# Causal self-attention in a two-layer decoder: reciprocals and maxima at later steps, and the mask of the second scores moved from TensorE to GpSimd

## The chip, the cores and the metric

The kernel runs on one core of one Trainium2 chip. The metric is the device time of one execution in microseconds (us), the median of three runs; less is better.

## The reference

Two decoder layers with normalisation behind each part, on x of 4 x 1024 x 256. Only the first part of the first layer is touched by the change: causal self-attention with 16 heads of 16 features.

```python
qkv = x @ w_in.T + b_in
q, k, v = split(qkv, 3)                       # 16 heads of 16
scores = einsum('bhqd,bhkd->bhqk', q / 4, k)
scores = scores + where(tril(ones((1024, 1024))), 0.0, -inf)
attn = softmax(scores)
out = einsum('bhqk,bhkd->bhqd', attn, v) @ w_out.T + b_out
x = layernorm(x + out)
```

Behind it come cross-attention, a quantised feed-forward block with a convolution, and the second layer (attention, cross-attention, feed-forward). They use other buffers and begin when the first part is done.

## The kernel before

The program is written engine by engine: inside each engine's function stands its own list of instructions in order, and semaphores tie the lists together. Each engine takes its instructions strictly in that order, so a wait holds all that stands behind it. SP (SyncE) issues all DMAs of this part.

**Groups, tiles and steps.** The 4 batches have 4 groups of 4 heads each: 16 groups. Sequence positions are cut in 8 tiles of 128. A group is gone through twice. The first pass (`first_scores`, L390 to L403) makes the scores of one query tile against all keys up to it in psA, adds a mask to the diagonal block by a product of identb and masku (L401), and VectorE takes the maximum of each row (L721, written negated to negm). The second pass (`second_scores`, L405 to L414) makes the scores of one key tile against all later queries in psB, with keys on the partitions; three additional rows of qst carry the negated maxima. ScalarE takes exp into pbuf (L535), and TensorE multiplies with V (`values`, L416 to L432) into psO, where an additional column of ones gives the denominators. psA, psB and psO have two halves each; pbuf has two buffers, one for odd and one for even key tiles.

A common step number k runs from 0 to 138 on all engines. Step k does a first-pass query tile of group k // 8, the second-pass key tile of step s = k - 10, and the product with V of the key tile of s - 1. Key tiles come in the order 3, 2, 1, 0, 7, 6, 5, 4, so that steps with k % 8 = 2 have key tile 3, those with k % 8 = 7 key tile 6, with k % 8 = 0 tile 5, with k % 8 = 1 tile 4. A step is made of rounds: one unit of second scores (up to 512 columns), some first scores, and in round 0 or 1 a product with V. c is the half of the queries (0 to 511, 512 to 1023) that a product is for.

**The mask of the second pass.** Where key tile and query tile are the same, queries ahead of the key must not see it. L413 adds to that block of 128 x 128 the product of identb and maskl, which is -1e30 there, so that exp makes zeros: one matmul for each head and key tile, 512 in all.

**Maxima.** At the end of each step with k % 8 = 7 TensorE transposes the maxima of the group (L477), VectorE splits them into three bfloat16 parts (`split_max`, L647 to L655), and SP stores them (L335) and loads them as rows of qst (L337). The second pass of the group begins at k % 8 = 2.

**Denominators.** At step 8g + 19 SP runs `reciprocals(g)` (L257 to L275): it stores the denominators of group g out of OT, moves OT to OTC, loads the denominators spread over 128 partitions, waits for VectorE's reciprocal (L687, on VectorE at step 8g + 20), stores the inverses and loads them broadcast to rden (four DMAs, L274). For odd g GpSimd multiplies OTC with rden (L573) at step 8g + 21.

**Other work in these steps.** The projections to q and k of the next batch (`qk_unit`: even steps 2 to 16 of 32; TensorE L368, ScalarE L508 and L514, GpSimd L558 to L566, SP L239), the projection to V (steps 24 to 31 of 32), the output projection of the batch before with residual and statistics (`out_unit`, steps 16 to 23 of 32; GpSimd L579 and L580), and GpSimd's rounding of the feed-forward weights (`quantise`, steps 18 to 28), on which SP's loads of later weights (L301 to L308, step 31) wait.

## Time and profile before

| | |
|---|---|
| median of 3 runs | 2337.58 us (2334.3 to 2339.44) |
| profiled execution | 2344.96 us |
| its span in the trace | 2343.2 us |
| PE busy | 2013.2 us, 86% of the span |
| DVE busy | 1439.8 us, 61% |
| ACT busy | 1207.0 us, 52% |
| POOL (GpSimd) busy | 726.3 us, 31% |
| the part that is changed | from 0 to about 782 us of the span |

PE is TensorE, PEld its weight loads, DVE VectorE, ACT ScalarE, SP SyncE. A matmul's duration counts its way through the array, and matmuls on end overlap: what one costs in a row of them is the distance of their starts. In square brackets stands how long the engine was idle before, and what released it.

### The profile page before, as it was taken

Reading aid. Unit: us, or ns where it says so; the run is one execution under the profiler, and the core shown is the slowest. Engines: PE = TensorE matmul, PEld = TensorE weight load, DVE = VectorE, ACT = ScalarE, POOL = GpSimd, SP = SyncE. Lnnn points to the kernel's source line nnn. Section 1 sums busy time; section 2 is a strip of 40 time slices with the busy share of each in tenths; the row PEclk is TensorE's granted clock in tenths of the full one; section 3 lists DMA queues with packets and bytes.
Section 4 is the critical chain, followed back from the end, with each engine's and each line's share of the span. In section 5 each row is a group of like instructions: output and inputs, shape, how many; then the busy total and the mean of one; then the engine's idle time right before and its main releaser. Section 6 shows DMA issues by size and latency. Waiting matters only on the chain. (4 is left out here: it accounts for less than half of the span.)

```text
span 2343.2 us, 32739 instructions
## 1 busy us (share of the span) xinstructions
PE 2013.2 (86%) x11274; PEld 1122.7 (48%) x11274; DVE 1439.8 (61%) x2698; ACT 1207.0 (52%) x2758; POOL 726.3 (31%) x1040
## 2 busy tenths in 40 slices
PE   6899799889998589999999985989899967798886
PEld 3344344334342345555555553556566643344444
DVE  4665576566773365666887985494844345567655
ACT  2355445544655166555787781557642314364352
POOL 4251220120010200021553551384833322343323
PEclk8899999999998799999999998999999978899998
DMA  6536433543531200000111013110001156645321
GB/s 153 118 66 151 81 64 83 92 83 66 75 58 39 67 22 5 28 26 8 55 53 43 35 44 145 53 46 10 30 28 52 45 118 125 125 86 113 79 63 41
DMA packets 134471, 156.56 MB, mean 67 GB/s; under 512 B 38446, under 2 KB 104882, under 8 KB 134211
## 3 DMA queue, kind: packets, MB, share of 16 engines
q1 hardware_dynamic: 134306, 154.48, 28.7%
q8 instruction: 91, 1.49, 0.3%
q14 instruction: 74, 0.60, 0.1%
HBM read 99.16 MB, written 46.86 MB: 62 GB/s over the span
## 5 line engine op out<-in xcount | busy, mean ns | idle before, releaser
L535 ACT ACTIVATE pbuf_sb<-psB 128x512 f32<-128x512 f32 (+1 forms) x608 | 330.2, 573 | 267.5 <-PE psB L413 216.2
L721 DVE TENSOR_REDUCE negm_sb<-psA 128x1 f32<-128x640 f32 (+6 forms) x352 | 351.8, 1027 | 180.5 <-PE psA L401 173.6
L1263 ACT ACTIVATE pw_sb<-psA,nmx_sb 128x154 f32<-128x154 f32 x512 | 192.3, 390 | 133.3 <-DVE nmx_sb L1408 133.3
L410 PE MATMUL psB<-qst_sb,kst_sb 99*128 99x512 bf16 (+3 forms) x768 | 239.3, 342 | 16.7 <-issue 6.3
L399 PE MATMUL psA<-kst_sb,qst_sb 96*128 96x512 bf16 (+3 forms) x768 | 201.6, 339 | 26.3 <-DVE negm_sb L721 25.3
L1408 DVE TENSOR_REDUCE nmx_sb<-psA 128x4 f32<-128x616 f32 x128 | 102.0, 797 | 124.6 <-PE psA L1032 124.2
L427 PE MATMUL psO<-pbuf_sb,V_sb 128*32 128x512 f32 (+3 forms) x1536 | 166.2, 513 | 11.0 <-ACT OT_sb L521 8.9
L410 PEld LDWEIGHTS psB<-qst_sb,kst_sb 99*128 99x128 bf16 x768 | 76.1, 100 | 183.7 <-ACT pbuf_sb L535 127.4
L2940 DVE TENSOR_REDUCE negm_sb<-psA 128x2 f32<-128x320 f32 x256 | 116.3, 481 | 71.2 <-PE psA L2703 69.6
L2823 ACT ACTIVATE pb_sb<-psB 128x512 f32<-128x512 f32 x160 | 93.4, 600 | 117.8 <-PE psB L2713 113.3
L985 PE MATMUL psO<-XT_sb,wq_x_sb 128*128 128x512 f32 x256 | 121.0, 596 | 0.0
L2703 PE MATMUL psA<-kst_sb,qst_sb 97*128 97x160 bf16 x512 | 83.3, 250 | 42.4 <-DVE negm_sb L2940 34.6
L985 PE MATMUL psO<-wo_x_sb,ox_sb 128*128 128x256 f32 x512 | 117.3, 383 | 1.7 <-DVE famw_sb L1494 0.9
L2052 PE MATMUL psO<-va_sb,pat_sb 128*128 128x256 f32 x512 | 115.9, 379 | 1.0 <-DVE pat_sb L2493 1.0
L2052 PE MATMUL psA<-XT_sb,ka_sb 128*128 128x512 f32 x256 | 116.8, 599 | 0.0
L558 POOL TENSOR_TENSOR q_sb<-q_sb,parts_sb 128x512 f32<-128x512 f32 x32 | 37.8, 1181 | 242.9 <-ACT parts_sb L514 242.7
L2466 DVE TENSOR_REDUCE nma_sb<-psA 128x1 f32<-128x1024 f32 x32 | 39.1, 1222 | 117.5 <-PE psA L2052 117.5
L399 PEld LDWEIGHTS psA<-kst_sb,qst_sb 96*128 96x128 bf16 x768 | 70.6, 101 | 80.7 <-DVE negm_sb L721 43.3
L401 PE MATMUL psA<-masku_sb,identb_sb 128*128 128x128 bf16 x512 | 108.6, 226 | 0.0
L2052 PEld LDWEIGHTS psO<-va_sb,pat_sb 128*128 128x128 f32 x512 | 96.9, 190 | 22.6 <-issue 7.7
L1046 PE MATMUL psB<-ident_sb,pr_sb 128*128 128x128 f32 x512 | 83.6, 286 | 26.6 <-DVE pt_sb L1401 26.5
L985 PEld LDWEIGHTS psO<-wo_x_sb,ox_sb 128*128 128x128 f32 x512 | 97.4, 192 | 17.3 <-ACT ox_sb L1198 1.7
(306 smaller groups left out, 4317.3 us busy)
## 6 DMA issues: line engine op xcount, KB each, us to landing
qst_sb<-parts_dram SPq DMA_DIRECT2D x192, 128.0 KB, 4.5
parts_dram<-parts_sb SPq DMA_DIRECT2D x32, 384.0 KB, 2.6
kst_sb<-parts_dram SPq DMA_DIRECT2D x96, 128.0 KB, 7.6
OTC_sb<-OT_sb SPq DMA_DIRECT2D x128, 64.0 KB, 5.7
rden_sb<-dens_dram SPq DMA_DIRECT2D x128, 64.0 KB, 2.2
x_dram<-X_sb SPq DMA_DIRECT2D x64, 128.0 KB, 1.7
y_dram<-yw_sb SPq DMA_DIRECT2D x16, 512.0 KB, 2.8
Y_sb<-y_dram SPq DMA_DIRECT2D x16, 512.0 KB, 9.0
```

What stands on the lines that cost most here:

```text
L399: nc.tensor.matmul(psA[:, k, at + lo:at + hi], qst[0:QK_ROWS, gg % 3, h, j * P:(j + 1) * P], kst[0:QK_ROWS, gg % 3, h, lo:hi], start=True, ...
L401: last = nc.tensor.matmul(psA[:, k, at + w - P:at + w], identb[:, :], masku[:, :], start=False, stop=True)
L410: last = nc.tensor.matmul(psB[:, k, at:at + hi - lo], kst[0:MAX_ROWS, gg % 3, h, i * P:(i + 1) * P], qst[0:MAX_ROWS, gg % 3, h, lo:hi], st ...
L427: last = nc.tensor.matmul(psO[32 * h:32 * h + 32, c, lo - c * 512:hi - c * 512], V[:, b % 2, i, at:at + 32], pbuf[:, i % 2, h, lo:hi], sta ...
L535: nc.scalar.activation(pbuf[:, key % 2, heads[0]:heads[-1] + 1, lo:hi], psB[:, (nb.n - 1) % 2, 0:len(heads) * (hi - lo)] .rearrange("p (h ...
L721: nc.vector.tensor_reduce(out=negm[:, gg % 2, heads[0]:heads[-1] + 1, j], in_=psA[:, (na.n - 1) % 2, :].rearrange("p (h n) -> p h n", h=le ...
L985: last = nc.tensor.matmul(dst, lhsT(i), rhs(i), start=(i == 0), stop=(i == n - 1))
L1263: last = nc.scalar.activation(pw[:, m % 2, h, :], psA[:, m % 2, at:at + K], ACT.Exp, bias=nmx[:, m % 2, h:h + 1], accum_out=psx[:, m % 3, ...
L1408: nc.vector.tensor_reduce(out=nmx[:, m % 2, :].rearrange("p (b a) -> p a b", a=2), in_=psA[:, m % 2, :].rearrange("p (a n) -> p a n", a=2) ...
L2052: last = nc.tensor.matmul(dst, lhsT(i), rhs(i), start=(i == 0), stop=(i == n - 1))
L2823: nc.scalar.activation(pb1[:, v % 2, h, :], psB[:, (nb.n - 1) % 2, :], ACT.Exp).then_inc(b_free, 1)
L2940: nc.vector.tensor_reduce(out=negm1[:, gg % 2, 2 * half:2 * half + 2, j], in_=psA[:, 0, half * 512:half * 512 + 2 * KP].rearrange("p (a n) ...
```

## The change

Line numbers below are those of the old file. The change
- drops maskl and its 512 products (L413); GpSimd sets the future part of each diagonal block of pbuf to zero instead, one `affine_select` of 128 x 4 x 128 for each step of the second pass (`clear_future`, 128 in all, the first thing GpSimd does in a step), and the product with V that reads this block waits for it (`future_cleared`);
- puts the product with V for c = 1 in round 1 rather than 0 where its key tile is 4 to 7;
- puts the transpose of the maxima behind round 0 of the next step, and `split_max` at the beginning of the next step on VectorE;
- splits SP's `reciprocals`: the inverses are stored and loaded four steps later, behind the maxima of that step; VectorE's reciprocal goes two steps later, GpSimd's scaling three, the output projection two;
- cuts GpSimd's rounding of weights in pieces of 512 columns over the steps 18 to 29;
- has ScalarE copy psO to OT before it stores the projection to q and k.

```diff
@@ -125,7 +125,6 @@
     masku = sb("masku", [P, P], BF16, first_stage)
-    maskl = sb("maskl", [P, P], BF16, first_stage)
     qst = sb("qst", [P, 3, 4, S], BF16, first_stage)
@@ -166,6 +165,7 @@
     inv_stored, inv_loaded, ot_scaled = sem0("f_inv_stored"), sem0("f_inv_loaded"), sem0("f_ot_scaled")
+    future_cleared = sem0("f_future_cleared")
     var_ready, rstd_ready, x_ready, x_stored = sem0("f_var_ready"), sem0("f_rstd_ready"), sem0("f_x_ready"), sem0("f_x_stored")
@@ -208,7 +208,7 @@
         b, kk = k // 32 - 1, k % 32
-        return (b, kk - 16) if 0 <= b < B - 1 and 16 <= kk < 24 else None
+        return (b, kk - 18) if 0 <= b < B - 1 and 18 <= kk < 26 else None
@@ -219,6 +219,13 @@
                             + bool(v_unit(i)) + bool(out_unit(i)) for i in range(k))
+
+    def diagonal_exps(s):
+
+        i = KEY_ORDER[s % 8]
+        before = 8 + sum((len(second_units(KEY_ORDER[(k - LEAD) % 8])) if k >= LEAD else 0) + bool(qk_unit(k))
+                         for k in range(s + LEAD))
+        return before + sum(lo == i * P for _, lo, _ in second_units(i))
@@ -253,7 +260,7 @@
-            def reciprocals(gg):
+            def denominators(gg):
@@ -264,6 +271,9 @@
                 sp.dma_start(dens[:, :], dens_dram[0].rearrange("h (a n) -> (h a) n", a=P // 4)).then_inc(dens_loaded, 16)
+
+            def inverses(gg):
+
                 sp.wait_ge(inv_made, gg + 1)
@@ -296,7 +306,7 @@
-                sp.wait_ge(quantised, 2)
+                sp.wait_ge(quantised, 8)
                 for dst, name in ((wk_x0, "L0_xattn_WkT"), (wv_x0, "L0_xattn_WvT"), (wq_x0, "L0_xattn_WqT")):
@@ -329,20 +339,23 @@
                 if early_groups(k) is not None:
-                    reciprocals(early_groups(k))
+                    denominators(early_groups(k))
                 if k < UNITS and k % 8 == 7:
...
                                  max_dram[gg % 2].rearrange("a (h j) n -> a h (j n)", h=4)).then_inc(maxrows_loaded, 16)
+                if early_groups(k - 4) is not None:
+                    inverses(early_groups(k - 4))
                 if k >= 2 and out_unit(k - 2):
...
                     sp.dma_start(X0[:, :, :], t["x"][b].rearrange("(n p) d -> p n d", p=P)).then_inc(x_loaded, 16)
-            reciprocals(G * B - 1)
+            denominators(G * B - 1)
+            inverses(G * B - 1)
             for j in range(NT):
@@ -406,11 +419,9 @@
                 for a, h in enumerate(heads):
-                    at, diagonal = a * (hi - lo), lo == i * P
+                    at = a * (hi - lo)
                     last = nc.tensor.matmul(psB[:, k, at:at + hi - lo], kst[0:MAX_ROWS, gg % 3, h, i * P:(i + 1) * P],
-                                            qst[0:MAX_ROWS, gg % 3, h, lo:hi], start=True, stop=not diagonal)
-                    if diagonal:
-                        last = nc.tensor.matmul(psB[:, k, at:at + P], identb[:, :], maskl[:, :], start=False, stop=True)
+                                            qst[0:MAX_ROWS, gg % 3, h, lo:hi], start=True, stop=True)
                 last.then_inc(b_full, 1)
@@ -419,6 +430,8 @@
                 pe.wait_ge(b_free, seen)
+                if c == i // 4:
+                    pe.wait_ge(future_cleared, 8 * gg + KEY_ORDER.index(i) + 1)
                 if i == KEY_ORDER[0] and gg > 0:
@@ -430,6 +443,13 @@
                     last.then_inc(pv_done, 1)
+
+            def transpose_maxima(gg):
+
+                pe.wait_ge(a_free, na.n)
+                a = slot_a()
+                nc.tensor.transpose(psA[0:32, a, 0:P], negm[:, gg % 2, :, :].rearrange("p h j -> p (h j)"),
+                                    ident[:, :]).then_inc(a_full, 1)
@@ -454,8 +474,10 @@
                         first_scores(k // 8, first[f], query_tile(k))
-                    if u == 0 and s >= 1:
+                    if u == (KEY_ORDER[(s - 1) % 8] >= 4) and s >= 1:
                         values((s - 1) // 8, KEY_ORDER[(s - 1) % 8], exps_at[s - 1], 1)
+                    if u == 0 and k % 8 == 0 and 8 <= k <= UNITS:
+                        transpose_maxima(k // 8 - 1)
                     if u == 1 and s >= 1:
@@ -471,11 +493,6 @@
                     nc.tensor.matmul(psA[:, a, 0:2], ones[:, :], asum[:, :], start=True, stop=True).then_inc(a_full, 1)
-                if k < UNITS and k % 8 == 7:
-                    pe.wait_ge(a_free, na.n)
-                    a = slot_a()
-                    nc.tensor.transpose(psA[0:32, a, 0:P], negm[:, (k // 8) % 2, :, :].rearrange("p h j -> p (h j)"),
-                                        ident[:, :]).then_inc(a_full, 1)
                 if v_unit(k):
@@ -535,13 +552,13 @@
                                              .rearrange("p (h n) -> p h n", h=len(heads)), ACT.Exp).then_inc(b_free, 1)
-                if qk_unit(k):
-                    store_qk(*qk_unit(k))
                 if s >= 0:
...
                         copy_out(gg, 0)
+                if qk_unit(k):
+                    store_qk(*qk_unit(k))
             copy_out(G * B - 1, 1)
@@ -579,17 +596,23 @@
+            def clear_future(s):
+
+                key = KEY_ORDER[s % 8]
+                pool.wait_ge(b_free, diagonal_exps(s))
+                nc.gpsimd.affine_select(out=pbuf[:, key % 2, :, key * P:(key + 1) * P],
+                                        in_=pbuf[:, key % 2, :, key * P:(key + 1) * P], compare_op=ALU.is_ge, fill=0.0,
+                                        base=0, pattern=[[0, 4], [1, P]], channel_multiplier=-1).then_inc(future_cleared, 1)
+
             link(nc.gpsimd.memset(ones[:, :], 1.0))
             link(nc.gpsimd.memset(mhalf[:, :], -0.5))
-            for m in (ident, identb, masku, maskl):
+            for m in (ident, identb, masku):
                 link(nc.gpsimd.memset(m[:, :], 0.0))
...
                                          base=0, pattern=[[-1, P]], channel_multiplier=1))
-            link(nc.gpsimd.affine_select(out=maskl[:, :], in_=maskl[:, :], compare_op=ALU.is_ge, fill=MASKED,
-                                         base=0, pattern=[[1, P]], channel_multiplier=-1))
             link(nc.gpsimd.memset(V[:, :, :, 0:H * (HD + 1)].rearrange("p a j (h e) -> p (a j) h e", h=H)[:, :, :, HD:HD + 1], 1.0))
@@ -600,29 +623,33 @@
-            def quantise(step):
+            def quantise(step, piece):
...
                 raw = (w_raw1, w_raw2)[i]
+                dst = (w1q, w2q)[i][:, :, :].rearrange("p c n -> p (c n)")
                 if i == 0:
                     raw = raw.rearrange("p c n -> p (c n)")
-                if step == 0:
+                if step == 0 and piece == 0:
                     pool.wait_ge(m1_ready, 1)
+                part = slice(piece * 512, (piece + 1) * 512)
                 if step % 3 == 0:
-                    link(nc.gpsimd.tensor_scalar(raw, raw, rs1[:, i:i + 1], ROUND, ALU.mult, ALU.add))
+                    link(nc.gpsimd.tensor_scalar(raw[:, part], raw[:, part], rs1[:, i:i + 1], ROUND, ALU.mult, ALU.add))
                 if step % 3 == 1:
-                    link(nc.gpsimd.tensor_scalar(raw, raw, ROUND, 1.0, ALU.subtract, ALU.min))
+                    link(nc.gpsimd.tensor_scalar(raw[:, part], raw[:, part], ROUND, 1.0, ALU.subtract, ALU.min))
                 if step % 3 == 2:
-                    nc.gpsimd.tensor_scalar((w1q, w2q)[i][:, :, :].rearrange("p c n -> p (c n)"), raw, -1.0, None,
-                                            ALU.max).then_inc(quantised, 1)
-                    pool.wait_ge(quantised, i + 1)
+                    nc.gpsimd.tensor_scalar(dst[:, part], raw[:, part], -1.0, None, ALU.max).then_inc(quantised, 1)
+                    pool.wait_ge(quantised, 4 * i + piece + 1)
             for k in range(LAST + 1):
+                if LEAD <= k < LAST:
+                    clear_future(k - LEAD)
                 if qk_unit(k):
                     split_qk(*qk_unit(k))
-                if 18 <= k < 30 and k % 2 == 0:
-                    quantise((k - 18) // 2)
-                done = early_groups(k - 2) if k >= 2 else None
+                if 18 <= k < 30:
+                    for piece in (0, 1) if k % 2 == 0 else (2, 3):
+                        quantise((k - 18) // 2, piece)
+                done = early_groups(k - 5)
                 if done is not None and done % 2 == 1:
@@ -712,6 +739,8 @@
             for k in range(LAST + 1):
+                if k % 8 == 0 and 8 <= k <= UNITS:
+                    split_max(k // 8 - 1)
                 if k < UNITS:
@@ -726,10 +755,8 @@
                         weight_scales()
-                    if k % 8 == 7:
-                        split_max(gg)
-                if early_groups(k - 1) is not None:
-                    reciprocals(early_groups(k - 1))
+                if early_groups(k - 3) is not None:
+                    reciprocals(early_groups(k - 3))
                 if v_unit(k):
```

**GpSimd, second batch, steps 44 to 50, before.** Names: q_sb and parts_sb belong to the split of the q and k projection, OTC_sb<-OTC_sb,rden_sb is the scaling by the inverses.

```order
L558 TENSOR_TENSOR q_sb<-q_sb,parts_sb 128x512
L565 CAST parts_sb<-q_sb 128x512
L566 TENSOR_TENSOR parts_sb<-q_sb,parts_sb 128x512
L573 TENSOR_TENSOR OTC_sb<-OTC_sb,rden_sb 128x1024
L558 TENSOR_TENSOR q_sb<-q_sb,parts_sb 128x512
L565 CAST parts_sb<-q_sb 128x512
L566 TENSOR_TENSOR parts_sb<-q_sb,parts_sb 128x512
L558 TENSOR_TENSOR q_sb<-q_sb,parts_sb 128x512
L565 CAST parts_sb<-q_sb 128x512
L566 TENSOR_TENSOR parts_sb<-q_sb,parts_sb 128x512
```

The same place now:

```order
L603 AFFINE_SELECT pbuf_sb<-pbuf_sb 128x4x128 x2
L575 TENSOR_TENSOR q_sb<-q_sb,parts_sb 128x512
L582 CAST parts_sb<-q_sb 128x512
L583 TENSOR_TENSOR parts_sb<-q_sb,parts_sb 128x512
L590 TENSOR_TENSOR OTC_sb<-OTC_sb,rden_sb 128x1024
L603 AFFINE_SELECT pbuf_sb<-pbuf_sb 128x4x128 x2
L596 TENSOR_SCALAR std_sb<-mv_sb 128x1
L597 TENSOR_TENSOR rstd_sb<-std_sb,mhalf_sb 128x1
L603 AFFINE_SELECT pbuf_sb<-pbuf_sb 128x4x128
```

The scaling stood ahead of two splits and stands now behind them, in step 48; ahead of it stand the clears of key tiles 6 and 5, behind it that of key tile 4 (the first of the two).

**SP, third batch, from the denominators of a group to the maxima of the next but one, before:**

```order
L259 DMA dens_dram<-OT_sb 4x1024
L264 DMA OTC_sb<-OT_sb 16x1024 x4
L266 DMA dens_sb<-dens_dram 128x32
L268 DMA dens_dram<-dens_sb 128x32
L274 DMA rden_sb<-dens_dram 16x1024 x4
L239 DMA parts_dram<-parts_sb 128x3x512 x2
L335 DMA max_dram<-mpart_sb 32x3x128
L337 DMA qst_sb<-max_dram 3x4096
```

The same place now:

```order
L266 DMA dens_dram<-OT_sb 4x1024
L271 DMA OTC_sb<-OT_sb 16x1024 x4
L273 DMA dens_sb<-dens_dram 128x32
L246 DMA parts_dram<-parts_sb 128x3x512 x2
L345 DMA max_dram<-mpart_sb 32x3x128
L347 DMA qst_sb<-max_dram 3x4096
L278 DMA dens_dram<-dens_sb 128x32
L284 DMA rden_sb<-dens_dram 16x1024 x4
```

The store of the inverses and the loads of rden stood ahead of the stores of parts and of the maxima; they stand now behind both DMAs of the maxima.

**TensorE, about the transpose at the end of step 39, before** (psA<-ident_sb,negm_sb is the transpose, psO<-pbuf_sb,V_sb a product with V):

```order
L399 MATMUL psA<-kst_sb,qst_sb 128x256
L401 MATMUL psA<-masku_sb,identb_sb 128x128
L477 MATMUL psA<-ident_sb,negm_sb 32x128
L410 MATMUL psB<-qst_sb,kst_sb 128x384
L413 MATMUL psB<-maskl_sb,identb_sb 128x128
L427 MATMUL psO<-pbuf_sb,V_sb 32x256 x4
L410 MATMUL psB<-qst_sb,kst_sb 128x384
L413 MATMUL psB<-maskl_sb,identb_sb 128x128
L399 MATMUL psA<-kst_sb,qst_sb 128x384
```

The same place now:

```order
L412 MATMUL psA<-kst_sb,qst_sb 128x256
L414 MATMUL psA<-masku_sb,identb_sb 128x128
L440 MATMUL psO<-pbuf_sb,V_sb 32x128 x4
L423 MATMUL psB<-qst_sb,kst_sb 128x384
L451 MATMUL psA<-ident_sb,negm_sb 32x128
L423 MATMUL psB<-qst_sb,kst_sb 128x384
L412 MATMUL psA<-kst_sb,qst_sb 128x384
L414 MATMUL psA<-masku_sb,identb_sb 128x128
L412 MATMUL psA<-kst_sb,qst_sb 128x384
```

The products with maskl are gone, the product with V of key tile 7 stands ahead of the transpose, and one unit of second scores does too; that of key tile 6 (32x256) stands behind the second unit.

## Rows read from the trace of the kernel before

**Rows 1.** Windows: the pass over all groups. Columns: stretch, us, engines' busy us, PE clock, DMA

```profile
90.00:770.00 680.00, 609.52 (x4283) 269.83 (x4282) 410.28 (x552) 368.70 (x679) 122.89 (x121) 0.96 0.38 75
```

**Rows 2.** Waits, 90 to 770 us: TensorE's weight loads held by ScalarE's exps

```profile
PEld psB L410 <- ACT pbuf_sb L535: 127.4, 280, 1.2
```

**Rows 3.** Timeline of PE, 16 matmuls on end: start, us, engine, line [idle before]

```profile
570.52 0.22 PE L410 MATMUL psB<-qst_sb,kst_sb 99*128 99x128 bf16 x1
...
571.40 0.22 PE L401 MATMUL psA<-masku_sb,identb_sb 128*128 128x128 bf16 x1
```

**Rows 4.** Timeline of PE: first matmuls behind DVE's four late reciprocals

```profile
239.26 1.03 PE L399 MATMUL psA<-kst_sb,qst_sb 96*128 96x512 bf16 x2 [3.62 <-DVE negm_sb L721]
...
290.24 1.03 PE L399 MATMUL psA<-kst_sb,qst_sb 96*128 96x512 bf16 x2 [5.55 <-DVE negm_sb L721]
...
427.41 1.03 PE L399 MATMUL psA<-kst_sb,qst_sb 96*128 96x512 bf16 x2 [3.77 <-DVE negm_sb L721]
...
478.20 1.03 PE L399 MATMUL psA<-kst_sb,qst_sb 96*128 96x512 bf16 x2 [5.56 <-DVE negm_sb L721]
```

**Rows 5.** Windows: eight microseconds behind the first of them

```profile
238.00:246.00 8.00, 6.74 (x41) 3.25 (x41) 5.47 (x6) 1.68 (x3) 0.00 (x0) 0.60 0.27 84
```

**Rows 6.** Timeline of PE: transposes of the maxima (L477), four of 16

```profile
251.19 0.28 PE L477 MATMUL psA<-ident_sb,negm_sb 128*32 128x128 f32 x1 [1.32 <-DVE negm_sb L721]
...
302.28 0.35 PE L477 MATMUL psA<-ident_sb,negm_sb 128*32 128x128 f32 x1 [1.32 <-DVE negm_sb L721]
...
612.75 0.28 PE L477 MATMUL psA<-ident_sb,negm_sb 128*32 128x128 f32 x1 [1.32 <-DVE negm_sb L721]
...
647.29 0.28 PE L477 MATMUL psA<-ident_sb,negm_sb 128*32 128x128 f32 x1 [1.32 <-DVE negm_sb L721]
```

**Rows 7.** Timeline of PE: product with V behind the copy of OT

```profile
218.31 1.07 PE L427 MATMUL psO<-pbuf_sb,V_sb 128*32 128x512 f32 x8 [1.68 <-ACT OT_sb L521]
...
589.59 0.64 PE L427 MATMUL psO<-pbuf_sb,V_sb 128*32 128x512 f32 x4 [0.42 <-ACT OT_sb L521]
```

**Rows 8.** Timeline of SP and POOL: maxima's and inverses' DMA issues, one scaling

```profile
614.25 0.32 SPq L335 DMA_DIRECT2D max_dram<-mpart_sb  x1
615.71 0.24 SPq L337 DMA_DIRECT2D qst_sb<-max_dram  x1
...
286.80 0.35 SPq L268 DMA_DIRECT2D dens_dram<-dens_sb  x1
288.25 1.72 SPq L274 DMA_DIRECT2D rden_sb<-dens_dram  x4
...
291.87 2.35 POOL L573 TENSOR_TENSOR OTC_sb<-OTC_sb,rden_sb 128x1024 f32<-128x1024 f32 x1 [7.51 <-DMA rden_sb<-dens_dram]
```

**Rows 9.** Timeline of PE: product of key tile 4 with V, after the transpose at 612.75

```profile
619.18 1.07 PE L427 MATMUL psO<-pbuf_sb,V_sb 128*32 128x512 f32 x8
```

**Rows 10.** Groups of POOL by form, 0 to 850 us: busy us, mean ns, idle before

```profile
L565 POOL CAST parts_sb<-q_sb 128x512 bf16<-128x512 f32 x24 | 14.7, 611 | 1.6
...
L587 POOL TENSOR_SCALAR_AFFINE_SELECT ident_sb<-ident_sb 128x128 f32<-128x128 f32 x1 | 0.3, 294 | 0.2 <-POOL maskl_sb L585 0.2
```

**Rows 11.** Timeline, 247 to 252 us: ScalarE's bias add, GpSimd's last split step

```profile
247.94 0.69 ACT L508 ACTIVATE q_sb<-psB,bqk_a_sb 128x512 f32<-128x512 f32 x1 [4.18 <-PE psB L368]
...
251.27 1.16 POOL L566 TENSOR_TENSOR parts_sb<-q_sb,parts_sb 128x512 bf16<-128x512 f32 x1
```

**Rows 12.** Timeline of SP and PE about the later weights' loads

```profile
192.38 0.58 SPq L301 DMA_DIRECT2D wk_x_sb<-L_xattn_WkT  x1
...
203.79 2.00 SPq L335 DMA_DIRECT2D max_dram<-mpart_sb  x1
...
210.08 0.23 PE L410 MATMUL psB<-qst_sb,kst_sb 99*128 99x128 bf16 x1 [0.97 <-DMA qst_sb<-max_dram]
```

**Rows 13.** Timeline of POOL and DVE, 76.9 to 78.2 us

```profile
76.92 1.15 POOL L566 TENSOR_TENSOR parts_sb<-q_sb,parts_sb 128x512 bf16<-128x512 f32 x1
...
76.95 1.26 DVE L655 TENSOR_TENSOR mpart_sb<-mrest_sb,mpart_sb 32x128 bf16<-32x128 f32 x1
```

## The prediction

> **What bounds the kernel now.** I read the windows first, then the chain and groups of waits, then the timelines of TensorE, SyncE and GpSimd about the places where the change puts something. In the stretch where all 16 groups pass, TensorE is busy 610 of 680 us, VectorE 410, ScalarE 369, GpSimd 123 [rows 1]: TensorE is the bound, and what shortens its list, or an idle time of its own, shortens the part by as much. The part ends before anything else of the kernel begins, so a microsecond won there is one won at the end. The remaining 70 us are idle in small pieces. 280 of TensorE's waits are for an exp that frees its half of psB [rows 2], 127.4 us by the weight loads' count, of which most lies beside matmuls still in flight; they say that ScalarE is close behind. The rest are pieces of 1 to 6 us in known places, below. A group without projections lasts 647.29 - 612.75 = 34.54 us from transpose to transpose [rows 6]; one group is the measure for all that follows.
>
> **What is taken away.**
>
> *The mask products.* A 128-column matmul on end costs 0.88 / 15 = 0.059 us, though it lasts 0.22 [rows 3]. 512 of them are 30 us: the upper end. The lower end is nothing, if each microsecond is waited for exps instead. In the steps of key tiles 5, 4 and 3 the exps follow each other closely, in the others TensorE has units of its own to do. I take about half, 1.0 us for a group, **-16**.
>
> *The late reciprocals.* Four times TensorE waits for a maximum that stands behind VectorE's reciprocal, which waits for the denominators: 3.62, 5.55, 3.77, 5.56, together 18.5 us [rows 4]. The reciprocal comes two steps later now, a quarter of a group, 34.54 / 4 = 8.6 us; the longest of these waits is 5.56 beside TensorE's own slack, so I let all go. Late next would be the inverses, below. Behind such a wait the granted clock is 0.60 for eight microseconds [rows 5], against 0.96 over the stretch [rows 1]. What that costs: from transpose 251.19 to 302.28 are 51.09 us [rows 6]; take off 34.54 for a plain group, 7.6 for the four projection units that an even group has beside it (1.9 each, an estimate from my reading of the matmuls), the idle 5.55 and one transpose's 1.32, and 2.1 remain. About 1.0 for the short ones: 6.2. Together **-24.7**.
>
> *ScalarE's order.* Behind a projection the product with V waits 1.68 us for the copy of OT, elsewhere 0.42 [rows 7]. The copy is first now: 4 x 1.26 = **-5.0**.
>
> *The transpose.* TensorE waits 1.32 us for the last maximum, 16 times [rows 6]. One product with V and one unit of scores stand ahead of it now, about 0.9 us. But the exps, which were ahead, get no earlier, so I take 0.4 for each group and 0.9 for the three that have the projection to V: **-9** (0 to -20).
>
> Sum: -54.8.
>
> **What is added.**
>
> *GpSimd's clears.* 128 affine_selects of 128 x 4 x 128. The nearest rows are a cast of as many elements, 0.61, and an affine_select of 128 x 128, 0.294 [rows 10]. If its fixed part is 0.1, four blocks are 0.1 + 4 x 0.195 = 0.88; between 0.61 and 4 x 0.294 = 1.18 all is possible. 128 x 0.88 = 113 us more on an engine with 557 us free. Behind an exp a clear has the rest of a step before its product, which the move to round 1 helps; that is the cover, and I set those that find GpSimd free at nothing. It has two holes.
>
> *The first hole: the scaling.* SP issues the inverses behind both DMAs of the maxima. Let T be the transpose. The maxima's store is issued at T + 1.50 (614.25 - 612.75 [rows 6, 8]), the load of qst 1.46 later. Then comes the store of the inverses, 0.3 behind it, 1.45 more until the loads of rden are issued, and 3.62 from there to the scaling (291.87 - 288.25) [rows 8]: T + 8.33. The scaling lasts 2.35 [rows 8]: T + 10.7. Behind it on GpSimd stands the clear of key tile 4, 0.98 with its hand-over: **T + 11.7**. TensorE asks for this block's product at T + 6.43 before (619.18 - 612.75 [rows 6, 9]), with one unit put ahead of it T + 7.1. So it stands for 4.6 us, and everything behind it with it, since it takes its list in order. This happens for each odd group but the last, seven times; where the projection to q and k lies in the step the wait is 4.1. Six times are some 27 us. The seventh, in step 32, is longer: the rounding of the weights now ends later in GpSimd's list, SP's loads of later weights wait for it (192.38), the maxima's store stands behind them (203.79), and its load already holds TensorE for 0.97 [rows 12]. With GpSimd's pieces ending some 3.4 us later I put 10 there. Together **+37**; rivals F and S hold its lower and upper end. The path is the chain of transfers, so TensorE coming earlier only lengthens its wait.
>
> *The clock behind it.* Seven stalls of 4 us and more, each like those of [rows 4]; with 1.5 us each (between the 1.0 and 2.1 above): **+10.5**.
>
> *The second hole: the split of a projection.* ScalarE's bias add takes 0.69 and GpSimd's last split step 1.16 [rows 11]; a whole split keeps GpSimd for 3.1 us and stands behind the clear of its own step, ahead of that of the next. Where the next product comes soonest, in steps 14, 38 and 70, I put 2.4 us each, in steps 16, 40 and 72 1.3 each: **+11**. Others end in time by a few tenths.
>
> Sum: +58.5. What remains I cost at nothing. VectorE's split moves with the transpose, and its 270 idle us [rows 1] cover it. The output projection brings the same instructions two steps later, on SP too (the load of its x and the stores of its y), behind which nothing stands that TensorE wants before the next maxima; it begins two steps behind the scaling, whose lateness the stall above already holds. The rounding in pieces lies in GpSimd's 557 idle us outside step 32; without that cover a piece would cost a clear behind it about 0.6, a cast of 512 [rows 10].
>
> **The net** is +3.7 us on the profiled execution's 2344.96 us, 2348.7. The median of the runs is 7.4 below that execution, so I forecast 2337.58 + 3.7, about **2341**. Two large sums of opposite sign make it: the range must be wide.
>
> **Two rules beside the rows.** VectorE's last step of the split, from two SBUF operands, took 1.26 us beside a GpSimd product of 1.15 us that began 0.03 earlier [rows 13]. The Trainium skill, "SBUF — State Buffer", section "Who interferes with whom", says that a VectorE instruction with two SBUF inputs and a GpSimd instruction that reads SBUF exclude each other. The trace agrees in this one place, and rival C is what it would do.
>
> The Trainium skill, "GPSIMD Engine Reference", section "3.1 Elementwise — side-by-side cycle accounting", gives 769 ns as the best case for 512 elements in a partition. By that a clear would be 0.1 shorter than I take, and the seven stalls shorter by 0.7 in all: the forecast would be 2340.
>
> **The rivals.**
>
> **A, the forecast: the two sums cancel.** 2341, of its own accord 2326 to 2356: the masks 7 us either way, the other terms 8. Chance 0.42.
>
> **S, slower: the scaling comes later still.** The loads of rden are issued behind the large load of qst and share the transfer engines with it. If each stall is 5.9 rather than 4.55, and its clock 2.0 rather than 1.5, this is 6 x 1.35 + 7 x 0.5 = 11.6 us, and with 2 more in step 32 the time is about 2354. It decides from T + 13 for the clear of key tile 4. For it: GpSimd's 7.51 us of waiting there already [rows 8]. Against it: those loads had other traffic too. Chance 0.19.
>
> **F, faster: TensorE gets all.** With the masks out of the way rounds close up, the 280 waits [rows 2] do not grow, and the full 30 us are won, 14 more than I take; and the inverses land early enough that a stall is 2.1 instead of 4.6: 6 x 2.5 = 15 less, and 5 less of clock. That is 2341 - 34 = 2307, between 2300 and 2318. It needs a scaling that begins by T + 5.8. For it: an idle SP between its two DMAs, and 3.62 us from issue to scaling, in which four loads queue and not one. Against it: the store of the inverses can't be issued before the load of qst. Chance 0.30.
>
> **C, the engines' common port.** 113 us of clears lie beside VectorE's work, which is busy 60% of the time [rows 1], so some 68 us overlap. If a sixth of that is waited for by TensorE, through maxima and splits, the time is 12 more: 2353. Against it: maxima read PSUM. Chance 0.05.
>
> **N, the change doesn't do what it says:** the denominators are still late for the reciprocal, and the 24.7 us stay: 2366. Chance 0.04.
>
> **The numbers.** 0.2% (4.7 us) is about what a measurement of this kernel can tell from no change: 2333 to 2342. F (0.30) is faster; of A (0.42) I give 0.11 to faster, 0.19 to same and 0.12 to slower, by where its range lies against these bounds; S, C and N (0.28) are slower. So faster 0.41, same 0.19, slower 0.40. The range leaves out the lower third of F (0.10) and N with some of S (0.08): 2306 to 2362.
>
> **What the profile of the changed kernel would show.** Right: TensorE's idle times of [rows 4] gone, no VectorE wait for the denominators above 1 us; some 29 us fewer of TensorE's busy time, with part of it back as waits for exps; seven idle times of 4 to 6 us of TensorE ahead of a product with V, released by the affine_select, each behind a scaling that ends near T + 10.7, and a low clock behind them; clears of 0.6 to 1.2 us. Wrong, to the fast side: those seven are under 2.5 us or released by something else, and the waits for exps are no longer than before. Wrong, to the slow side: clears above 1.2 us, or waits for them in every group, even ones too. If the total is right but the seven stalls are missing, the two sums were both wrong.

## The result, and the profile after

| | before | changed |
|---|---|---|
| median of 5 runs | 2337.58 us (2334.30 to 2339.44) | 2348.90 us (2343.49 to 2354.14) |
| ratio to before, 95% interval | | 1.0047 [1.0033, 1.006] |
| profiled execution, its span | 2344.96, 2343.2 | 2343.49, 2341.8 |
| start of the last output projections (end of the part) | 781.38 | 774.22 |

The changed kernel is slower by 0.47%, 11 us; 2341 was forecast, in a range of 2306 to 2362. The profiled executions alone would say the opposite: that of before was 7.4 us above its median, that of the changed kernel was the fastest of its five. So sums are compared below by medians and ratios, and the traces are used for what happens where. A percentage is turned into microseconds with the 2337.58 us of the kernel before.

TensorE's waits in the changed kernel, 90 to 770 us. Columns: what waited, for what; us in total, times, longest us. The first group is PE itself, the last is the weight loads:

```profile
PE psO L440 <- POOL pbuf_sb L603: 45.3, 16, 6.4
PE psA L451 <- DVE negm_sb L750: 6.2, 9, 0.7
...
PE psB L423 <- DMA qst_sb<-max_dram: 5.1, 3, 3.9
PE psA L451 <- DVE X_sb L696: 4.4, 3, 1.5
...
PE psO L440 <- ACT OT_sb L538: 2.5, 5, 0.8
...
PE psA L412 <- DVE negm_sb L750: 1.2, 7, 0.2
...
PEld psB L423 <- ACT pbuf_sb L552: 120.5, 266, 1.2
```

45.3 us of a wait that didn't exist before, for the affine_select (L603). What was to go has mostly gone: waits for a maximum ahead of first scores (L412) are 1.2 us in all, where four of [rows 4] alone were 18.5; the transpose (L451) waits 0.7 at most for a maximum, where it was 1.32 [rows 6], but three transposes now wait 1.45 each for VectorE's residual of the output projection (X_sb, L696), which the forecast had at nothing; the copy of OT costs 2.5 us, 8.9 before. The weight loads' waits for exps are about what they were in [rows 2], 120.5 us for 127.4.

Seven of those 16 waits are long. TensorE's timeline of the changed kernel, the matmuls behind each:

```profile
215.47 1.94 PE L440 MATMUL psO<-pbuf_sb,V_sb 128*32 128x512 f32 x8 [5.67 <-POOL pbuf_sb L603]
...
304.20 1.91 PE L440 MATMUL psO<-pbuf_sb,V_sb 128*32 128x512 f32 x8 [3.33 <-POOL pbuf_sb L603]
...
393.31 1.93 PE L440 MATMUL psO<-pbuf_sb,V_sb 128*32 128x512 f32 x8 [5.55 <-POOL pbuf_sb L603]
...
482.01 1.94 PE L440 MATMUL psO<-pbuf_sb,V_sb 128*32 128x512 f32 x8 [3.30 <-POOL pbuf_sb L603]
...
570.97 1.94 PE L440 MATMUL psO<-pbuf_sb,V_sb 128*32 128x512 f32 x8 [5.45 <-POOL pbuf_sb L603]
...
644.08 1.93 PE L440 MATMUL psO<-pbuf_sb,V_sb 128*32 128x512 f32 x8 [6.22 <-POOL pbuf_sb L603]
...
725.43 1.93 PE L440 MATMUL psO<-pbuf_sb,V_sb 128*32 128x512 f32 x8 [6.38 <-POOL pbuf_sb L603]
```

They sum to 35.9 us. The chain behind the fifth, first TensorE's transpose:

```profile
558.88 0.28 PE L451 MATMUL psA<-ident_sb,negm_sb 128*32 128x128 f32 x1 [0.35 <-DVE V_sb L688]
```

then SP's issues and GpSimd's work, from the changed kernel's timelines:

```profile
560.38 0.33 SPq L345 DMA_DIRECT2D max_dram<-mpart_sb  x1
561.86 0.26 SPq L347 DMA_DIRECT2D qst_sb<-max_dram  x1
562.17 0.34 SPq L278 DMA_DIRECT2D dens_dram<-dens_sb  x1
564.12 1.70 SPq L284 DMA_DIRECT2D rden_sb<-dens_dram  x4
...
567.77 2.34 POOL L590 TENSOR_TENSOR OTC_sb<-OTC_sb,rden_sb 128x1024 f32<-128x1024 f32 x1 [5.55 <-DMA rden_sb<-dens_dram]
570.18 1.22 POOL L603 TENSOR_SCALAR_AFFINE_SELECT pbuf_sb<-pbuf_sb 128x512 f32<-128x512 f32 x2
```

This answers to [rows 8]. Counted from T = 558.88: maxima stored at T + 1.50, qst loaded at + 2.98, inverses stored at + 3.29, rden loaded at + 5.24, scaling at + 8.89, its end at + 11.2, the product at + 12.1. Two clears stand behind the scaling in a row (x2 in 1.22 us): the second is the next step's, which was ready by then. TensorE had been waiting since 570.97 - 5.45 = 565.52, T + 6.6.

A clear by itself, the line's own view:

```profile
L603 POOL TENSOR_SCALAR_AFFINE_SELECT pbuf_sb<-pbuf_sb x128: 632/636/642, 87.0 to 759.1; 128x512 f32<-128x512 f32 x128
```

0.636 us each, 81 us in all, without any spread. And three windows of the changed kernel (us, busy PE, PEld, DVE, ACT, POOL, PEclk, DMA share, GB/s): eight microseconds behind the fifth stall, one plain group without a stall, and eight microseconds behind the seventh stall:

```profile
571.50:579.50 8.00, 7.37 (x50) 2.50 (x43) 3.76 (x5) 4.21 (x8) 0.64 (x1) 0.85 0.75 111
...
598.00:631.00 33.00, 30.56 (x225) 11.98 (x225) 25.39 (x29) 21.19 (x41) 5.09 (x8) 1.00 0.47 68
...
725.40:733.40 8.00, 6.93 (x31) 1.16 (x31) 0.00 (x0) 3.08 (x6) 0.47 (x1) 0.50 0.12 20
```

That group lasts 631.22 - 598.17 = 33.05 us from transpose to transpose, against 34.54 in [rows 6]: 1.5 us won for a group, where 1.0 for masks and 0.4 for the transpose were reckoned. The group that ends 47.6 us after 631.22 (42.5 before) holds the sixth stall and loses more than that.

### The profile page after: what moved, and what is told of

Its sections match the earlier page's. It is cut to its first block and busy times, and to the rows that moved or that the text cites. A ratio compares the mean times of both kernels' runs of the same rounds, so it can differ in the third digit from the quotient of the medians.

```text
span 2341.8 us, 31985 instructions
## 1 busy us (share of the span) xinstructions
PE 1983.6 (85%) x10762; PEld 1090.7 (47%) x10762; DVE 1442.0 (62%) x2698; ACT 1201.6 (51%) x2758; POOL 808.3 (35%) x1184
## 5 line engine op out<-in xcount | busy, mean ns | idle before, releaser
L423 PE MATMUL psB<-qst_sb,kst_sb 99*128 99x512 bf16 (+3 forms) x768 | 219.4, 340 | 29.2 <-issue 10.1
L440 PE MATMUL psO<-pbuf_sb,V_sb 128*32 128x512 f32 (+3 forms) x1536 | 170.5, 524 | 51.6 <-POOL pbuf_sb L603 45.3
L412 PE MATMUL psA<-kst_sb,qst_sb 96*128 96x512 bf16 (+3 forms) x768 | 197.1, 333 | 8.0 <-DVE negm_sb L750 7.1
L603 POOL TENSOR_SCALAR_AFFINE_SELECT pbuf_sb<-pbuf_sb 128x512 f32<-128x512 f32 x128 | 80.9, 636 | 245.9 <-ACT pbuf_sb L552 245.1
L423 PEld LDWEIGHTS psB<-qst_sb,kst_sb 99*128 99x128 bf16 x768 | 63.6, 98 | 205.3 <-ACT pbuf_sb L552 120.5
L1290 ACT ACTIVATION_READ_ACCUMULATOR pw_sb<-psA,nmx_sb 128x1 f32 x512 | 105.2, 205 | 0.0
```

Source lines behind the costliest of these rows:

```text
L412: nc.tensor.matmul(psA[:, k, at + lo:at + hi], qst[0:QK_ROWS, gg % 3, h, j * P:(j + 1) * P], kst[0:QK_ROWS, gg % 3, h, lo:hi], start=True, ...
L423: last = nc.tensor.matmul(psB[:, k, at:at + hi - lo], kst[0:MAX_ROWS, gg % 3, h, i * P:(i + 1) * P], qst[0:MAX_ROWS, gg % 3, h, lo:hi], st ...
L440: last = nc.tensor.matmul(psO[32 * h:32 * h + 32, c, lo - c * 512:hi - c * 512], V[:, b % 2, i, at:at + 32], pbuf[:, i % 2, h, lo:hi], sta ...
L1290: last = nc.scalar.activation(pw[:, m % 2, h, :], psA[:, m % 2, at:at + K], ACT.Exp, bias=nmx[:, m % 2, h:h + 1], accum_out=psx[:, m % 3, ...
```

## The experiments

The time of each is the median of 4 to 12 runs. The ratio is to the kernel before, run beside it on the same chip, with its interval at 95%. Runs 1 to 4, 5 to 8, 9 to 11 and 12 stand in four series, so two of different series are compared by their ratios, which adds the uncertainty of both.

**1. The inverses ahead of the maxima** (the changed kernel, SP):

```diff
+                if early_groups(k - 4) is not None:
+                    inverses(early_groups(k - 4))
                 if k < UNITS and k % 8 == 7:
                     sp.wait_ge(maxparts_made, gg + 1)
...
-                if early_groups(k - 4) is not None:
-                    inverses(early_groups(k - 4))
```

> The changed kernel, but SP issues the inverses in the same step ahead of the two DMAs of the maxima. Theory (the seven stalls come from the place of the inverses on SP): the affine_select of key tile 4 no longer stands behind a late scaling, the seven idle times of 3.3 to 6.4 us of TensorE (35.9 us in the changed kernel's trace) fall under 1.5 us each, some 7 to 10 us of clock come back with them: 2349 - 43, about 2306 (2300 to 2314). Rival 1 (the 2.3 us of the scaling itself or the clears hold TensorE wherever the inverses land): idle before the product of key tile 4 stays above 2 us each, time above 2325. Rival 2 (the inverses are not yet made there, so the maxima come later): waits for qst of several us in place of the stalls, time 2335 to 2350.

2311.6 us, ratio 0.9892 [0.9874, 0.991]. Its waits, 90 to 760 us:

```profile
PE psO L440 <- POOL pbuf_sb L603: 14.9, 11, 3.0
PE psB L423 <- DMA qst_sb<-max_dram: 12.0, 6, 7.3
```

By ratios this is 1.55% under the changed kernel, 36 us, for two lines moved on one queue. The long waits for the clear are gone but for 2.96 and 2.34 in the two stalled steps that hold a split of a projection. Part of rival 2 is in it: in two places the maxima now come late, and the waits for qst are 12.0 us where they were 5.1. So 36 us is what the stalls cost less what this repair costs itself. TensorE there:

```profile
212.37 1.03 PE L423 MATMUL psB<-qst_sb,kst_sb 99*128 99x128 bf16 x5 [7.28 <-DMA qst_sb<-max_dram]
...
258.47 1.03 PE L423 MATMUL psB<-qst_sb,kst_sb 99*128 99x128 bf16 x5 [2.50 <-DMA qst_sb<-max_dram]
```

**2. The scaling a step later, SP's order as changed**:

```diff
-                done = early_groups(k - 5)
+                done = early_groups(k - 6)
```

> The changed kernel, but GpSimd scales one step later, behind the clear of key tile 4; SP's order is left as changed. Theory (a late scaling is harmful only for what stands behind it): the stalls at key tile 4 go; the clear of key tile 3 stands behind the scaling now, which ends about 10.7 us behind the transpose, about when its product is asked for, so at most 1 us is left at each of seven places: 2306 to 2315. Rival (the transfers themselves, or the stalls' place in the list, are not it): the idle moves one step on at 3 us or more each, time above 2330.

2309.8 us, 0.9881 [0.9862, 0.99]: 1.66% under the changed kernel, 39 us. The transfers come as late as in the changed kernel, but only one clear stands behind the scaling, in time. In all, waits for clears are 9.4 us, the longest 1.8. One wait of more than 3 us is new, but it is for the scaled values themselves, in an output projection:

```profile
622.63 1.93 PE L381 MATMUL psA<-wo_a_sb,OTC_sb 128*128 128x256 f32 x4 [3.23 <-POOL OTC_sb L590]
```

What makes the stall is thus a late instruction ahead of a clear in GpSimd's list; either end of the pair can be moved.

**3. No mask at all in the kernel before** (the mask of the second pass is left out):

```diff
-                    if diagonal:
-                        last = nc.tensor.matmul(psB[:, k, at:at + P], identb[:, :], maskl[:, :], start=False, stop=True)
```

> The kernel before without the 512 mask products of the second pass; the mask of the second pass is left out, nothing takes its place. Theory (TensorE's list is the bound but exps are close behind): 14 to 18 us less, 2320 to 2324. Rival F (all of the products' 0.059 us is won): 29 us less, 2308. Rival (exps pace these steps): no change, 2337.

2328.0 us, 0.9961 [0.9945, 0.9977]: 9 us, less than reckoned. A plain group is 635.67 - 602.04 = 33.6 us against 34.5, 0.9 us as taken, and other groups without a late reciprocal win up to 1.6; but in those with one the gain does not arrive. TensorE's timeline of this run, two transposes and the late maximum between them:

```profile
246.83 0.28 PE L475 MATMUL psA<-ident_sb,negm_sb 128*32 128x128 f32 x1 [1.32 <-DVE negm_sb L719]
...
286.67 1.03 PE L399 MATMUL psA<-kst_sb,qst_sb 96*128 96x512 bf16 x2 [5.92 <-DVE negm_sb L719]
...
298.15 0.28 PE L475 MATMUL psA<-ident_sb,negm_sb 128*32 128x128 f32 x1 [1.32 <-DVE negm_sb L719]
```

This group lasts 51.3 us, and did 51.1 in [rows 6], with 32 products less in it: its wait for the reciprocal went from 5.55 to 5.92. The four groups that hold such a wait last 198.5 us in sum, and 198.8 before. The longer wait is not the whole reason, for the four waits are 17.1 us here and 18.5 in [rows 4]. The granted clock is lower too: 0.90 over this group and over the one ahead of it, where the kernel before has 0.93 over both, and over whole runs it is 0.9445 on the mean of 12, where the kernel before has 0.9492 on that of 17. How much each takes is not shown.

**4. The move of the reciprocals alone** (mask products kept): denominators and inverses split as in the change, and

```diff
-                if early_groups(k - 1) is not None:
-                    reciprocals(early_groups(k - 1))
+                if early_groups(k - 3) is not None:
+                    reciprocals(early_groups(k - 3))
...
-                done = early_groups(k - 2) if k >= 2 else None
+                done = early_groups(k - 5)
```

> The kernel before with the move of the reciprocals alone (inverses four steps later behind the maxima, VectorE's reciprocal two, GpSimd's scaling three, output projection two); mask products and all else as before. Theory: the four idle times of TensorE behind the reciprocals (18.5 us) and the clock behind them (6.2) go and nothing waits for the scaling, which has no clear behind it: 2313 (2309 to 2320). Rival (the wait moves on, to the projection of the output or to the split of a projection behind the scaling): less than 12 us won, above 2325.

2315.5 us, 0.9903 [0.9886, 0.992]: 22.7 us won. With the same late scaling, on the same queues, there is no stall; no clear stands behind it here. The longest wait of TensorE for GpSimd in it is 1.8 us, for the scaled values themselves.

**5. The clears alone** (masks replaced by clears, rounding in pieces, product in round 1; reciprocals and maxima as before):

```diff
-                    if diagonal:
-                        last = nc.tensor.matmul(psB[:, k, at:at + P], identb[:, :], maskl[:, :], start=False, stop=True)
...
+                if c == i // 4:
+                    pe.wait_ge(future_cleared, 8 * gg + KEY_ORDER.index(i) + 1)
...
+                if LEAD <= k < LAST:
+                    clear_future(k - LEAD)
```

> The kernel before with the masks replaced by GpSimd's clears alone (the rounding in pieces and the product with V in round 1 with it); reciprocals, maxima, copy and output projection as before. Theory (a clear is harmful only behind something late, and the old scaling comes in the steps of key tiles 0 and 1): what the mask products give (9 us by the run without them) less the holes behind the split of a projection (9 us): 2337 (2331 to 2343), no idle time of over 3 us released by an affine_select. Rival (clears stall in every order, for the scaling waits for its inverses there too): 2350 or more, idle times of 3 us and more ahead of products with V of key tile 7.

2335.5 us, 0.9995 [0.9981, 1.0009]: no change, the clears take back the 9 us that the dropped products are worth alone. Its waits:

```profile
PE psO L435 <- POOL pbuf_sb L594: 8.5, 10, 1.8
PE psB L418 <- DMA qst_sb<-max_dram: 3.9, 2, 3.3
```

The waits for clears, 8.5 us, are the 9 reckoned there, and the old place of the scaling has none. The 3.3 us for qst stand at 207.33, step 32: with the rounding cut in pieces the later weights, and the maxima behind them, come later.

**6. ScalarE's copy first, alone:**

```diff
-                if qk_unit(k):
-                    store_qk(*qk_unit(k))
                 if s >= 0:
                     if i == 0 and gg > 0:
                         copy_out(gg - 1, 1)
                     if i == 5:
                         copy_out(gg, 0)
+                if qk_unit(k):
+                    store_qk(*qk_unit(k))
```

> The kernel before with ScalarE's copy of OT ahead of its bias adds, nothing else. Theory: the four waits of 1.68 us fall to 0.4, 5 us: 2332 (2330 to 2336). Rival (the bias adds are now late for GpSimd's split and SP's stores, or the psB half they free is late): no change or more, 2337 to 2341.

2337.8 us, 1.0006 [0.9994, 1.0018]: nothing. The four waits of 1.68 us for the copy are gone; TensorE's timeline shows where they went:

```profile
234.50 1.04 PE L399 MATMUL psA<-kst_sb,qst_sb 96*128 96x512 bf16 x2 [5.04 <-DVE negm_sb L721]
...
285.01 1.03 PE L399 MATMUL psA<-kst_sb,qst_sb 96*128 96x512 bf16 x2 [7.31 <-DVE negm_sb L721]
...
419.97 1.03 PE L399 MATMUL psA<-kst_sb,qst_sb 96*128 96x512 bf16 x2 [5.16 <-DVE negm_sb L721]
...
473.13 1.03 PE L399 MATMUL psA<-kst_sb,qst_sb 96*128 96x512 bf16 x2 [7.51 <-DVE negm_sb L721]
```

Against [rows 4] the waits behind the late reciprocals are longer by 1.42, 1.76, 1.39 and 1.95: 6.5 us, nearly the 6.7 of the four waits of 1.68 that went. The end of that wait is set by transfers, not by TensorE: ahead of the denominators SP stores the parts of a projection and loads the next stack of q and k. From the issue of that store to VectorE's reciprocal pass 237.77 - 220.93 = 16.84 us in the kernel before and 233.01 - 216.50 = 16.51 here, while TensorE begins to wait 14.71 us behind the store before and 12.96 here.

**7. The transpose and VectorE's split later, alone:**

```diff
+                    if u == 0 and k % 8 == 0 and 8 <= k <= UNITS:
+                        transpose_maxima(k // 8 - 1)
...
-                if k < UNITS and k % 8 == 7:
-                    pe.wait_ge(a_free, na.n)
...
+                if k % 8 == 0 and 8 <= k <= UNITS:
+                    split_max(k // 8 - 1)
```

> The kernel before with the transpose of the maxima behind round 0 of the next step and VectorE's split at the beginning of it, nothing else. Theory: the 15 waits of 1.32 us shrink to what the exps allow, 9 us: 2328 (2322 to 2333). Rival F (all of it is won): 2317. Rival (the maxima reach qst later and TensorE waits for those): no gain, 2337, with waits for qst.

2330.0 us, 0.9973 [0.9962, 0.9984]: 6.3 us. The transposes' waits for a maximum fall from 19.8 us to 3.3. The second rival is in it in part: waits for qst are 5.1 us in four places, 1.3 before. The longest of them:

```profile
207.71 0.23 PE L410 MATMUL psB<-qst_sb,kst_sb 99*128 99x128 bf16 x1 [3.02 <-DMA qst_sb<-max_dram]
```

This is step 32, where [rows 12] has 0.97 and the changed kernel 3.87. The rounding is whole here, so two of the three microseconds added there come from the later transpose and not from the pieces.

**8. The changed kernel without clears** (the mask of the second pass is left out):

```diff
-                if LEAD <= k < LAST:
-                    clear_future(k - LEAD)
...
-                if c == i // 4:
-                    pe.wait_ge(future_cleared, 8 * gg + KEY_ORDER.index(i) + 1)
```

> The changed kernel without its clears, so that the mask of the second pass is left out, and TensorE waits for none. Theory (the cost of the change is its clears' holes): 45 us of stalls and some 10 us of clock go: 2294 (2287 to 2302). Against the run with the inverses first it tells what the clears still cost there: by the theory the 9 us behind splits, the rival being that GpSimd's 81 us also slow VectorE, which would make it 2285 or less.

2285.5 us, 0.9784 [0.977, 0.9797], faster than reckoned. This is the sum of all that the change takes away: 2.16%, 50.5 us. The rest, 1.0047 - 0.9784 = 2.63% or 61.5 us, is the price of 128 clears in the place where the change puts them. The time is also what the rival names (VectorE slowed by the clears, 2285 or less), and against run 1 the clears cost 1.08%, 25 us, and not 9. Run 1's own waits account for that: 14.9 us for clears and 12.0 for qst, where this run has none and 1.2. Run 12 bounds the rival: it has all 128 clears and is 6.5 us slower than this run, so VectorE's slowing costs no more than that.

**9 to 12. Towards a version that beats both.** First the split of a projection behind the next step's clear too (scaling as in 2):

```diff
-                if qk_unit(k):
-                    split_qk(*qk_unit(k))
+                if k >= 1 and qk_unit(k - 1):
+                    split_qk(*qk_unit(k - 1))
```

> The changed kernel with the scaling one step later and, besides, GpSimd's split of a projection one step later, so that it too stands behind the clear of its step. Theory (the second hole is the split ahead of a clear): against the run with the scaling alone later (2310) the nine waits of TensorE for an affine_select (9.4 us) go, and of the 24 us that separate it from the run without clears some 10 come back: 2300 (2295 to 2304). Rival (what separates them is in ScalarE's and TensorE's own waits and the clear's time behind an exp): no change, 2308 to 2312. Rival (the parts reach SP and the stacks later): slower, 2315.

2306.6 us, 0.9867 [0.9844, 0.989]. Waits for clears fall to 3.8 us, but the time only by 0.14% against 2, and the intervals overlap. Something stands in its trace that takes the gain back:

```profile
PE psA L381 <- POOL OTC_sb L590: 7.6, 3, 2.9
PE psO L440 <- POOL pbuf_sb L603: 3.8, 5, 1.8
```

The first output projection of each of three batches waits for the scaling, which was made a step later; in run 2 one did, for 3.2 us. So 5.6 us of waits for clears went and 4.4 of these came.

The change without its clears, mask products kept (reciprocals, transpose, copy and output projection moved, GpSimd's rounding whole); what it lacks of the change:

```diff
-            def clear_future(s):
...
+                    if diagonal:
+                        last = nc.tensor.matmul(psB[:, k, at:at + P], identb[:, :], maskl[:, :], start=False, stop=True)
...
-                    if u == (KEY_ORDER[(s - 1) % 8] >= 4) and s >= 1:
+                    if u == 0 and s >= 1:
```

> The change without its clears: reciprocals, transpose, copy and output projection moved as in the changed kernel, the 512 mask products kept. Theory (the parts add where no clear stands behind the scaling): 2337 - 22 - 6 = 2309 (2305 to 2313), as much as the repaired versions with clears give. Rival (the parts overlap, since both free TensorE at the same steps): 2315 or more. Rival (the copy helps only once the others are gone): 2304.

2307.1 us, 0.9868 [0.9849, 0.9888]. The parts alone make 0.9903 x 0.9973 x 1.0006 = 0.9882: they add up, and the copy's place is worth some 3 us with them, which lies within the intervals. The whole change but for its clears is 31 us faster than before. Against run 8 (0.9784) the 512 mask products are worth 0.84%, 20 us, where no reciprocal is late; alone they gave 9. (The two runs differ also in the rounding and in the place of the product with V, and stand in different series.) The rest of the 30 us shows in part as waits: the weight loads' waits for exps are 136.4 us without the products and 127.4 with them.

The later weights behind the maxima, on top of 9:

```diff
-                if k == 31:
+                if k == 33:
                     late_weights()
```

> The run with split and scaling later, and SP's loads of the later weights two steps later, behind the maxima of step 31. Theory (at step 32 the maxima's store stood behind weights that wait for the rounding): the one wait of 4 us for qst goes, 2296 if the other is 2300. Rival (the loads now collide with the inverses of the same steps): no gain.

2304.2 us, 0.9856 [0.9834, 0.9878]. No wait for qst is longer than 0.8 us any more; in time the two cannot be told apart. Last, the output projection a step later on all engines:

```diff
-        return (b, kk - 18) if 0 <= b < B - 1 and 18 <= kk < 26 else None
+        return (b, kk - 19) if 0 <= b < B - 1 and 19 <= kk < 27 else None
```

> The run with split, scaling and later weights moved, and the output projection one step later on all engines. Theory (with the scaling a step later TensorE's first output projection of a batch waits for it, 7.6 us in three places): those waits go, ratio to the kernel before about 0.982, 2297. Rival (the output projection then meets the projection to V in one more step and VectorE is late for both): no gain, 0.9856.

2292.9 us, 0.9812 [0.9788, 0.9835], as the theory has it: 44 us or 1.9% under the kernel before, and within 7 us of run 8, which leaves the mask of the second pass out. Two of GpSimd's scalings and TensorE's only remaining waits for GpSimd in it, from their timelines:

```profile
156.09 1.08 PE L440 MATMUL psO<-pbuf_sb,V_sb 128*32 128x256 f32 x8 [1.08 <-POOL pbuf_sb L603]
...
678.82 1.94 PE L440 MATMUL psO<-pbuf_sb,V_sb 128*32 128x512 f32 x8 [0.18 <-POOL pbuf_sb L603]
...
710.69 1.06 PE L440 MATMUL psO<-pbuf_sb,V_sb 128*32 128x512 f32 x8 [1.76 <-POOL pbuf_sb L603]
```

```profile
540.10 2.36 POOL L590 TENSOR_TENSOR OTC_sb<-OTC_sb,rden_sb 128x1024 f32<-128x1024 f32 x1 [2.53 <-DMA rden_sb<-dens_dram]
606.73 2.36 POOL L590 TENSOR_TENSOR OTC_sb<-OTC_sb,rden_sb 128x1024 f32<-128x1024 f32 x1 [3.73 <-DMA rden_sb<-dens_dram]
```

There is one more wait for a clear, of 0.46 at 704.88. The scaling still waits for its inverses, and nobody pays for it.

## Why the prediction was right, point by point

| term | forecast | by the runs |
|---|---|---|
| all gains | -54.8 | -50.5 (run 8) |
| reciprocals | -24.7 | -22.7 (4) |
| mask products | -16 (0 to -30) | -9 alone (3), -20 with the rest moved (8 against 10) |
| transpose | -9 | -6 (7) |
| copy | -5 | 0 alone (6) |
| all losses | +58.5 | +61.5 (changed against 8) |
| scaling ahead of key tile 4's clear, with its clock | +47.5 | +36 and +39 net of what the repairs cost (1, 2) |
| split ahead of clears | +11 | five waits of 1.2, 6 us; 3 in time, with new waits against it (9 against 2) |

**The main mechanism held.** Seven stalls ahead of the product of key tile 4, behind a scaling that waits for inverses that stand behind the maxima on SP. That the stall comes from this pair of places is shown by the runs that undo one side each: the clears alone cost no more than the products that they replace (5), the late scaling alone nothing that shows (4), both together 36 us or more, and the stalls go with either repair (1, 2), but for 5.3 us in run 1. The parts taken alone would make 0.9903 x 0.9973 x 0.9995 x 1.0006 = 0.9877; the whole is 1.0047.

**What the two rows of losses leave open.** 36 to 39 and 3 are 39 to 42, not 61.5. Each repair costs something itself. Run 1 keeps 5.3 us of the stalls and waits 6.9 us more for qst; run 2 waits 3.2 for an output projection. With these added back the stalls and their clock come to 42 to 48 us, an estimate, where 47.5 was put. From run 2 to run 12 another 0.69%, 16 us, comes back by the split, the later weights and the output projection together, and 6.5 remain to run 8. How much of the 16 belongs to the split alone is not shown. Its waits are not where the forecast had the larger ones: none stands in steps 14, 38 and 70 (2.4 each), and 1.2 each in steps 16, 40, 48, 72 and 80. Another 1.4 us stand in step 24 behind the pieces of the rounding, which were put at nothing.

**Sizes of the stall.** The wait was put at 4.55, and 4.1 with a projection; it was 5.45 to 6.38 and 3.3. The chain was later by 0.5 at the loads of rden and so at the scaling (T + 8.9 for T + 8.3), TensorE earlier by half a microsecond, which together make the fifth one's 0.9. In the sixth the loads took longer (4.42 us from issue to scaling, 3.65 in the fifth); in the seventh they did not (3.71), but TensorE asked earlier, at T + 5.8. With a projection the scaling begins at T + 10.5 (301.01 - 290.51); the split stands ahead of it, but the scaling still waits 0.32 us for its inverses, whose loads SP issues at T + 6.85 there. TensorE comes later by more, at T + 10.4 (304.20 - 3.33 - 290.51). In step 32 the wait for qst was 3.87 and the stall 5.67: 9.5 where 10 was put. Seven stalls make 35.9, qst some 3 more than before; 37 was forecast. The reason given for step 32 is right only in part. In the kernel before, the rounding had ended at 161.5 and the loads of the later weights at 192.38 waited for nothing; in the changed kernel they wait until 192.76 for it. But run 7, whose rounding is whole, has 3.02 of the 3.87 us, of which 0.97 stood there before: two thirds of what was added come from the later transpose, which the forecast did not reckon there. That 10 came near to 9.5 is partly luck.

**The clock behind them was not overpriced as far as can be seen.** 1.5 us each was taken from stretches at a granted clock of 0.60 [rows 5], a window that begins 1.26 us ahead of the matmul, in the wait. Eight microseconds that begin with the matmul have 0.69, 0.67, 0.71 and 0.68 behind the four late reciprocals of before, and 0.78, 0.79, 0.80, 0.80, 0.82, 0.69 and 0.50 behind the seven stalls. The length of the wait doesn't tell which: 3.30 us and 5.55 are both followed by 0.80, 6.22 by 0.69 and 6.38 by 0.50. If TensorE bounds all of these windows, the seven cost 14.6 us, an estimate of the upper end (8 us times what the clock lacks to 1); 10.5 was put. The repairs can't separate it, as both have waits of their own.

**The gains were misjudged by parts.** The step that failed is "the copy is first now: 4 x 1.26 = -5.0", and with it half of the masks' 16: each was reckoned as if the waits of [rows 4] stood still beside it. But those end at a transfer's time. For the copy run 6 shows that what TensorE wins ahead of them it waits there; for the masks the waits and the lower clock of run 3 share it. In the whole change they are gone, and there masks and transpose give what a plain group shows, 1.5 us. The wrong single prices did little harm to the sum, in part by luck: the copy and the transpose bring some 5 us less than was put, the masks 4 more. One price came out by a slip that cancels: for the low clock behind a reciprocal the prediction takes a transpose's 1.32 us off, which stands in the plain group too, and leaves out the copy's 1.26, which doesn't.

**Where the 7.6 us between 2341 and 2348.9 lie.** Gains 4.3 short, losses 3 too small; no term of its own is behind it. Rival S named the right side: the plain stalls were longer by 0.9 to 1.8 us than the forecast's, those with a projection shorter by 0.8, and a heavier clock stands behind the last two only. Rival F would have needed a scaling by T + 5.8; the earliest came at T + 8.9. Its first half, that the masks give the full 30 us, is not borne out either: 20, nearer to the 16 that were put.

**Rival C is real and free.** VectorE's last step of the split of the maxima has two SBUF operands. Two of them from VectorE's timeline of the changed kernel, one alone and one beside a clear:

```profile
200.21 0.28 DVE L682 TENSOR_TENSOR mpart_sb<-mrest_sb,mpart_sb 32x128 bf16<-32x128 f32 x1
...
249.71 0.61 DVE L682 TENSOR_TENSOR mpart_sb<-mrest_sb,mpart_sb 32x128 bf16<-32x128 f32 x1
```

Seven of 16 take 0.61 to 0.74 there; without clears (run 8) all take 0.28 but the first (0.70), which stands beside a split. Six times a third of a microsecond are 2 us on VectorE, and the chain of the stalls doesn't lengthen by it: where such a slow step stands ahead of one (transposes at 290.51 and 468.35), SP issues the load of qst at T + 4.16, and in run 8 with the fast step at T + 4.18 and 4.20. The Trainium skill, "SBUF — State Buffer", section "Who interferes with whom", has such a pair exclude each other; these durations agree. The reductions of the maxima, whose operand is in PSUM, kept theirs (1.22 us for 1024 columns in both).
